# A selective-scan layer and a linear-attention layer: softplus chain and du moved three slots, diagonals of B through DRAM, one state's inflow on GpSimd

## Chip, cores and metric

The kernel runs on one core of one Trainium2 chip. The metric is the device time of one execution in microseconds (us). Below, PE is TensorE, DVE is VectorE, ACT is ScalarE, POOL is GpSimd and SP is SyncE, whose queue issues most DMAs.

## The reference

The input x is [2, 512, 64, 64] in float32, two images of 4096 tokens with 512 channels. Two layers follow each other; each takes the group norm of x, computes a layer of it and adds x again. The first is a Mamba layer with 1024 inner channels, 16 states and a rank of 32 for delta. Only its core matters here:

```python
x_dbl = xs @ x_proj_w.T                       # xs: [tokens, 1024], after conv and SiLU
dt, Bm, Cm = x_dbl[..., :32], x_dbl[..., 32:48], x_dbl[..., 48:]
delta = softplus(dt @ dt_proj_w.T + dt_proj_b)
A = -exp(A_log)                               # [1024, 16]
def step(h, inp):                             # over the 4096 tokens
    dA = exp(d_t[..., None] * A)
    dBu = (d_t * u_t)[..., None] * b_t[:, None, :]
    h = dA * h + dBu
    y = einsum('bdn,bn->bd', h, c_t)
y = (y + u * D_skip) * silu(z)
```

The second layer is a linear attention of 8 heads. The change does not touch it.

## The kernel before

**Chunks, tiles, slots.** The first layer goes over the tokens in 16 chunks of 512. A chunk is made of 8 tiles (j, 128 inner channels each), and a tile of 16 states (n). One state of one tile is a slot, so a chunk has 128 slots. The functions `scalar_chunk`, `vector_chunk`, `gpsimd_chunk`, `tensor_chunk` and `sync_chunk` write the queue of their engine slot by slot; the engines then run freely and meet at semaphores. Three things are laid over one another: the scan of chunk c, the front of chunk c+1 (norm, input projection, convolution, the projection to dt, B and C) and the output projection of chunk c-1. The tables of numbers at the head of the file (`OUT_MM`, `IN_MM`, `SP_LN`, `DU`, ...) say in which slot each piece stands. Chunks 1 to 14 run all three in a loop; chunk -1 is a front alone, chunk 0 has no output projection, chunk 15 has no front.

**A slot of the scan.** ACT makes the decay exp(delta * A) two slots ahead (L444). The inflow delta * u * B is made in one of two ways. For the ten states of `BY_TENSOR`, PE multiplies the transposed delta * u (`du_t`) with a diagonal matrix that holds the state's row of B (`b_diag`), four 128x128 matmuls into one of three PSUM banks, also two slots ahead (L742); a matmul of this type is two records in the profile, so a group is eight. For the six states of `BY_VECTOR`, DVE multiplies a copy of du with the broadcast row `b_rows` (L647), and then the decay goes to the PSUM bank. DVE scans (L659) into a ring of four buffers `hs`; POOL multiplies with `c_rows` into a ring of four buffers `hc` (L704); PE adds the sixteen products up by transposing matmuls three slots later (L846).

**The three banks.** `ring_bank(n)` deals the banks to the slots. Two other uses take a turn in the ring: the sum over the states of the tile before, transposed back (`Y_BACK`, L718), after slot `Y_AFTER`, and the transpose of du (`DU_TURN`, L725), after slot `DU_AFTER`. Behind such a turn the bank of a slot was free one scan later than else: `scans_before` gives 2 in place of 3, which for slot n means that its producer, two slots ahead, waits for the end of scan n-2 and not n-3. With `DU_AFTER` = 13 these are the slots 6, 7 (PE's groups) and 14, 15 (ACT's decays).

**The softplus chain.** During tile j the delta of tile j+1 is made: ACT Abs and Relu in slot 0, Exp in 1, two additions in 2 and 3 (`SP_ROUND`), POOL subtracts in 4 (`SP_REST`, L672), ACT takes Ln in 6 (`SP_LN`, L536, with a load of ACT's function table before it and another before the next decay), POOL adds in 8 (L676), subtracts in 9 (L681) and makes `du` in 10 (L690). PE transposes `du` in slot 12 (L725), ACT copies it to `du_t` in 13 (L540), and PE's groups for states 0 and 1 of tile j+1 stand in slots 14 and 15. `du_t` has two buffers.

**Rows and diagonals of B.** At slot 102 (`DBL`) ACT has B and C of the next chunk in `sq`. SP stores them to DRAM (L400) and loads them back, broadcast over the partitions, as `b_rows` (L408) and `c_rows` (L411), each row when its last user of the present chunk is done. For the diagonals PE transposes the rows (`B_TURN`, L751) and DVE multiplies an identity with them, one instruction a state, in the ten `BY_TENSOR` slots of tile 7 (L630).

Of the kernel before, what the change touches and what calls it, by code (L numbers as in the profile page):

```python
# [28 lines left out]
BY_TENSOR = (0, 1, 3, 4, 6, 7, 9, 10, 12, 13)  # L29
N_V, N_T = len(BY_VECTOR), len(BY_TENSOR)  # L30
# [3 lines left out]
Y_AFTER, DU_AFTER = 5, 13  # L34
# [94 lines left out]
def mamba_and_linear_attention(nc, x, ln_w, ln_b, in_proj, conv_w, conv_b, x_proj, dt_proj, dt_b, a_log, d_skip,  # L129
# [6 lines left out]
    bc_d = nc.dram_tensor("b_and_c_rows", [2 * STATE, T], FP32).ap()  # L136

    outer = ExitStack()
    with outer:
# [11 lines left out]
        with layer0:  # L151
# [1134 lines left out]
```

## Time and profile before

| | before |
|---|---|
| median of 3 runs | 5272.86 us (5270.67 to 5282.67) |
| the profiled execution | 5273.96 us, its span 5272.2 us |
| PE busy | 4649.4 us, 88% |
| DVE busy | 3947.5 us, 75% |
| POOL busy | 3635.1 us, 69% |
| ACT busy | 3497.5 us, 66% |
| first and last scan start | 186.0 us and 4479.9 us |

The sum of such shares hides the stages: up to 186 us stand the setup and the front of chunk 0, then 16 chunks of scan, and from about 4480 us the second layer. The start of a scan of state 0 marks a tile's beginning; the windows in the section of rows below are cut there.

### The profile page before, as it was taken

Reading aid. Unit: us, or ns where it says so; the run is one execution under the profiler, and the core shown is the slowest. Engines: PE = TensorE matmul, PEld = TensorE weight load, DVE = VectorE, ACT = ScalarE, POOL = GpSimd, SP = SyncE. Lnnn points to the kernel's source line nnn. Section 1 sums busy time; section 2 is a strip of 40 time slices with the busy share of each in tenths; the row PEclk is TensorE's granted clock in tenths of the full one; section 3 lists DMA queues with packets and bytes.
Section 4 is the critical chain, followed back from the end, with each engine's and each line's share of the span. In section 5 each row is a group of like instructions: output and inputs, shape, how many; then the busy total and the mean of one; then the engine's idle time right before and its main releaser. Section 6 shows DMA issues by size and latency. Waiting matters only on the chain. (4 is left out here: it accounts for less than half of the span.)

```text
span 5272.2 us, 90572 instructions
## 1 busy us (share of the span) xinstructions
PE 4649.4 (88%) x26392; PEld 3440.3 (65%) x26392; DVE 3947.5 (75%) x4317; ACT 3497.5 (66%) x6211; POOL 3635.1 (69%) x2906
## 2 busy tenths in 40 slices
PE   1798989898989898989898989999898988798998
PEld 0566666666666666666666666666666667586786
DVE  4788979898988888888888898989798988212212
ACT  1676767676767676777777777767676766463663
POOL 1477778777777777777777777777777789332432
PEclk8899999999999999999999999999999999999999
DMA  5102020201010201010101001010102010323313
GB/s 191 53 1 65 5 66 5 62 9 62 9 62 9 62 9 58 13 58 13 58 13 47 24 29 41 20 49 13 58 4 67 4 59 7 116 64 104 104 56 112
DMA packets 119824, 245.61 MB, mean 47 GB/s; under 512 B 10496, under 2 KB 11648, under 8 KB 117728
## 3 DMA queue, kind: packets, MB, share of 16 engines
q1 hardware_dynamic: 110816, 222.30, 12.9%
q10 hardware_dynamic: 8448, 16.78, 0.9%
q8 instruction: 237, 3.88, 0.3%
q14 instruction: 323, 2.65, 0.2%
HBM read 204.44 MB, written 34.60 MB: 45 GB/s over the span
## 5 line engine op out<-in xcount | busy, mean ns | idle before, releaser
L704 POOL TENSOR_TENSOR hc<-hs,c_rows 128x512 f32<-128x512 f32 x2048 | 2598.1, 1278 | 931.9 <-DVE hs L659 456.7
L659 DVE TENSOR_TENSOR_SCAN hs<-da,carry,bank 128x512 f32<-128x512 f32 x1280 | 1630.9, 1274 | 213.7 <-PE bank L742 110.4
L742 PE MATMUL bank<-b_diag,du_t 128*128 128x128 f32 x10240 | 1425.2, 284 | 282.3 <-ACT du_t L540 183.9
L742 PEld LDWEIGHTS bank<-b_diag,du_t 128*128 128x128 f32 x10240 | 1287.6, 197 | 347.4 <-issue 178.2
L846 PEld LDWEIGHTS bank<-identity,hc 128*128 128x128 f32 x8192 | 1016.9, 144 | 664.4 <-issue 558.3
L846 PE MATMUL bank<-identity,hc 128*128 128x128 f32 x8192 | 1251.3, 277 | 17.0 <-ACT sp_l L548 12.3
L444 ACT ACTIVATE da<-delta,neg_a 128x512 f32<-128x512 f32 x1280 | 906.1, 716 | 192.0 <-DVE hs L659 190.4
L659 DVE TENSOR_TENSOR_SCAN hs<-bank,carry,hs 128x512 f32<-128x512 f32 x768 | 962.3, 1266 | 0.5
L444 ACT ACTIVATE bank<-delta,neg_a 128x512 f32<-128x512 f32 x768 | 526.3, 685 | 555.0 <-DVE hs L659 443.0
L1017 POOL TENSOR_TENSOR xg_low<-xg,xg_high 128x512 fp32r<-128x512 f32 x192 | 248.5, 1295 | 473.3 <-ACT xg_high L1041 465.7
L647 DVE TENSOR_TENSOR hs<-bank,b_rows 128x512 f32<-128x512 f32 x768 | 518.3, 675 | 73.2 <-POOL hc L704 56.1
L832 PE MATMUL bank<-xs,w_out 128*128 (+1 forms) x1024 | 534.7, 626 | 29.9 <-issue 27.6
L782 PE MATMUL bank<-xn,w_in 128*128 (+1 forms) x1024 | 525.1, 599 | 23.5 <-DVE xs L594 12.4
L814 PE MATMUL bank<-xn,w_in 128*128 (+1 forms) x1024 | 524.9, 594 | 0.0
L424 ACT ACTIVATE carry<-hs,keep_now 128x2 f32<-128x2 f32 x1008 | 292.6, 290 | 241.5 <-DVE hs L659 238.7
L588 DVE SCALAR_TENSOR_TENSOR bank<-raw,w_conv,bank 128x512 f32<-128x512 f32 x384 | 289.6, 754 | 96.3 <-ACT bank L495 87.2
L832 PEld LDWEIGHTS bank<-xs,w_out 128*128 128x128 f32 x1024 | 188.4, 201 | 190.0 <-issue 184.6
L672 POOL TENSOR_TENSOR sp_w<-sp_w,sp_e 128x512 f32<-128x512 f32 x128 | 163.3, 1276 | 159.6 <-ACT sp_w L532 159.5
L814 PEld LDWEIGHTS bank<-xn,w_in 128*128 128x128 f32 x1024 | 174.6, 191 | 123.0 <-issue 122.4
L1041 ACT ACTIVATE xg<-xl,gn_bias,gn_scale 128x512 f32<-128x512 f32 x192 | 155.4, 809 | 137.5 <-DMA xl<-x 125.3
L1130 DVE COPY ek_t<-l_bank 128x512 f32<-128x512 f32 x64 | 44.3, 692 | 219.2 <-PE l_bank L1205 219.2
L609 DVE SCALAR_TENSOR_TENSOR xs<-xs,skip,bank 128x512 f32 (+1 forms) x128 | 94.5, 739 | 143.5 <-PE bank L718 143.5
(160 smaller groups left out, 5882.5 us busy)
## 6 DMA issues: line engine op xcount, KB each, us to landing
c_rows<-b_and_c_rows SPq DMA_DIRECT2D x256, 256.0 KB, 3.5
xl<-x SPq DMA_DIRECT2D x48, 1024.0 KB, 5.6
b_rows<-b_and_c_rows SPq DMA_DIRECT2D x96, 256.0 KB, 3.6
c_rows<-in_x SPq DMA_DIRECT2D x8, 2048.0 KB, 8.2
xn<-in_x ACTq DMA_DIRECT2D x16, 1024.0 KB, 7.4
xres<-in_x SPq DMA_DIRECT2D x64, 256.0 KB, 3.1
x<-xres SPq DMA_DIRECT2D x64, 256.0 KB, 2.0
out<-keys SPq DMA_DIRECT2D x16, 1024.0 KB, 5.0
```

What stands on the lines that cost most here:

```text
L424: act.activation(carry[:, col:col + 2], hs[:, col % H_RING:col % H_RING + 2, T - 1], ACT.Copy, scale=keep_now[:, 0:1]).then_inc(carried, 1)
L444: act.activation(x_ps[ring_bank(nn)][:, :] if nn in BY_VECTOR else da[:, nn % X_RING, :], delta[:, jn % 2, :], ACT.Exp, scale=neg_a[:, jn, ...
L588: dve.scalar_tensor_tensor(in_ps[t][:, :], raw[:, TAPS - 1 - s:TAPS - 1 - s + T], w, in_ps[t][:, :], ALU.mult, ALU.add).then_inc(conv_step, 1)
L647: dve.tensor_tensor(hs[:, nn % H_RING, :], du_ps[:, :], b_rows[:, v, :], ALU.mult).then_inc(dbu_ready, 1)
L659: dve.tensor_tensor_scan(hs[:, n % H_RING, :], decay, inflow, carry[:, STATE * j + n:STATE * j + n + 1], ALU.mult, ALU.add).then_inc(h_rea ...
L704: pool.tensor_tensor(hc[:, n % HC_RING, :], hs[:, n % H_RING, :], c_rows[:, n, :], ALU.mult).then_inc(hc_ready, 1)
L742: mm = pe.matmul(x_ps[ring_bank(nn)][:, q * P:(q + 1) * P], du_t[:, jn % 2, q * P:(q + 1) * P], b_diag[:, w, q, :], start=True, stop=True)
L782: mm = pe.matmul(in_ps[t][:, :], w_in[:, ct, t * P:(t + 1) * P], xn[:, f % 2, ct, :], start=ct == 0, stop=ct == CT - 1)
L814: mm = pe.matmul(pb[:, :], w_in[:, ct, lo:lo + P], xn[:, c % 2, ct, :], start=ct == 0, stop=ct == CT - 1)
L832: mm = pe.matmul(pout[:, :], w_out[:, k, ct * P:(ct + 1) * P], xs[:, o % 2, k, :], start=k == 0, stop=k == JT - 1)
L846: mm = pe.matmul(y_ps[:, q * P:(q + 1) * P], hc[:, ns % HC_RING, q * P:(q + 1) * P], identity[:, :], start=ns == 0 and q == 0, stop=ns == ...
L1017: pool.tensor_tensor(xg_parts[1][:, u, ct, :], xg[:, ct % 2, :], xg_parts[0][:, u, ct, :], ALU.subtract).then_inc(lowered, 1)
```

## The change

- `DU_AFTER` goes from 13 to 11. The chain moves: Exp of the softplus into slot 0, the additions into 1 and 2, POOL's subtraction into 3, Ln into 4, POOL's sum into 5, its second subtraction into 6, du into 8, PE's transpose of du into 10 and ACT's copy to `du_t` into 11. Ln now writes over `sp_e`, so it waits for POOL's subtraction, which reads `sp_e`; before it wrote `sp_l` and waited for the transpose of y. The SiLU gate of POOL goes from slot 7 to 9, the Tanh of z from 10 to 11. Slots 12 and 13 (PE's groups) now have the late bank, and 14 and 15 no longer.
- `du_t` has two buffers in both kernels; only the slot of the copy changes.
- The diagonals come by DMA. Setup zeroes `b_diag` on POOL and stores it as the blank of a DRAM tensor `b_diagonals`. Each chunk, SP writes the nine rows of B onto the diagonals in DRAM and loads the nine [128 x 512] blocks back. PE's turn (L751) and DVE's ten multiplications (L630) are gone.
- State 3 leaves `BY_TENSOR` for `BY_POOL`: POOL multiplies du with a broadcast row, two slots ahead, into the ring of `hs`, and the decay of state 3 goes to the bank.

```diff
 BY_VECTOR = (2, 5, 8, 11, 14, 15)
-BY_TENSOR = (0, 1, 3, 4, 6, 7, 9, 10, 12, 13)
+BY_TENSOR = (0, 1, 4, 6, 7, 9, 10, 12, 13)
+BY_POOL = (3,)
-Y_AFTER, DU_AFTER = 5, 13
+Y_AFTER, DU_AFTER = 5, 11
...
-    return 2 if Y_AFTER < n <= Y_AFTER + 2 or n > DU_AFTER else 3
+    return 2 if n - Y_AFTER in (1, 2) or n - DU_AFTER in (1, 2) else 3
...
-DT_MM, SP_ABS, SP_EXP, SP_ROUND, SP_LN, SP_REST, SP_SUM, SP_DELTA = 14, 0, 1, 3, 6, 4, 8, 9
-DU, DU_TURN, DU_T, DU_COPY = 10, DU_AFTER - 1, DU_AFTER, 15
-Z_MM, Z_TANH, Z_SILU = (2, 3, 6, 9), 10, 12
-Y_COPY, Y_BACK, Y_SKIP, Y_GATE = 3, Y_AFTER - 1, Y_AFTER + 1, 7
+DT_MM, SP_ABS, SP_EXP, SP_ROUND, SP_LN, SP_REST, SP_SUM, SP_DELTA = 14, 0, 0, 2, 4, 3, 5, 6
+DU, DU_TURN, DU_T, DU_COPY = 8, DU_AFTER - 1, DU_AFTER, 15
+Z_MM, Z_TANH, Z_SILU = (2, 3, 6, 9), 11, 12
+Y_COPY, Y_BACK, Y_SKIP, Y_GATE = 3, Y_AFTER - 1, Y_AFTER + 1, 9
...
+                    sp.wait_ge(diag_blank, 1)
+                    sp.dma_start(diag_d.rearrange("w q (p c) -> p (w q) c", p=P),
+                                 b_diag[:, :, :, :].rearrange("p w q c -> p (w q) c")).then_inc(diag_zeroed, 16)
...
                         sp.dma_start(bc_d, bc_rows).then_inc(bc_stored, 16)
+                        for w, n in enumerate(BY_TENSOR):
+                            wait(sp, diag_loaded[w], 16 * f)
+                            settle(sp, sp_fence)
+                            sp.dma_start(diag_d[w:w + 1, :, 0:P * P:P + 1],
+                                         bc_rows[n:n + 1, :].rearrange("a (q p) -> a q p", p=P),
+                                         allow_slow_non_contiguous=True).then_inc(diag_stored, 16)
                         sp.wait_ge(bc_stored, 16 * (f + 1))
                         settle(sp, sp_fence)
+                        sp.wait_ge(diag_stored, 16 * N_T * (f + 1))
...
+                            if n in BY_TENSOR:
+                                w = BY_TENSOR.index(n)
+                                wait(sp, dbu_mm, N_T * (JT * (c + 1) - 1) + w + 1)
+                                sp.dma_start(b_diag[:, w, :, :], diag_d[w].rearrange("q (p c) -> p q c", p=P)
+                                             ).then_inc(diag_loaded[w], 16)
...
                                 if n == SP_LN:
-                                    wait(act, y_back, tile)
-                                    act.activation(sp_l[:, :], sp_e[:, :], ACT.Ln, bias=one).then_inc(sp_ln, 1)
+                                    act.wait_ge(sp_rest, nt + 1)
+                                    act.activation(sp_e[:, :], sp_e[:, :], ACT.Ln, bias=one).then_inc(sp_ln, 1)
...
-                            if front and j == JT - 1 and n in BY_TENSOR:
-
-                                w = BY_TENSOR.index(n)
-                                dve.wait_ge(b_turned, f + 1)
-                                wait(dve, dbu_mm, N_T * (tile if scan else 0) + (w + 1 if scan else 0))
...
-                                dve.tensor_tensor(b_diag[:, w, :, :],
...
+                            if scan and n + 2 in BY_POOL:
+                                nn = n + 2
...
+                                pool.tensor_tensor(hs[:, nn % H_RING, :], du[:, :], b_rows[:, ROWS.index(nn), :],
+                                                   ALU.mult).then_inc(pool_dbu, 1)
```

PE's queue at the end of a tile of chunk 0, before. The groups of states 12 and 13 (`bank<-b_diag,du_t`) come first, then the transpose of du, a sum over the states (`bank<-identity,hc`), and the group of state 0 of the next tile:

```order
L742 MATMUL bank<-b_diag,du_t 128x128 x4
L846 MATMUL bank<-identity,hc 128x128 x4
L742 MATMUL bank<-b_diag,du_t 128x128 x4
L846 MATMUL bank<-identity,hc 128x128 x4
L725 MATMUL bank<-identity,du 128x128 x4
L846 MATMUL bank<-identity,hc 128x128 x8
L742 MATMUL bank<-b_diag,du_t 128x128 x4
L802 MATMUL bank<-dt_rows,w_dt 128x512
```

The same place of PE's queue in the changed kernel, where the groups are L775, the sums L870 and the transpose of du L760:

```order
L760 MATMUL bank<-identity,du 128x128 x4
L775 MATMUL bank<-b_diag,du_t 128x128 x4
L870 MATMUL bank<-identity,hc 128x128 x4
L775 MATMUL bank<-b_diag,du_t 128x128 x4
L870 MATMUL bank<-identity,hc 128x128 x12
L775 MATMUL bank<-b_diag,du_t 128x128 x4
L826 MATMUL bank<-dt_rows,w_dt 128x512
```

The transpose of du now stands ahead of the groups of states 12 and 13, and between them and the first group of the next tile stand three sums.

POOL's queue over one tile of chunk 0, before (`hc<-hs,c_rows` is the product of a slot, the others are the softplus chain, du and the gate `xs<-xs,zs`):

```order
L672 TENSOR_TENSOR sp_w<-sp_w,sp_e 128x512
L704 TENSOR_TENSOR hc<-hs,c_rows 128x512 x3
L697 TENSOR_TENSOR xs<-xs,zs 128x512
L704 TENSOR_TENSOR hc<-hs,c_rows 128x512
L676 TENSOR_TENSOR delta<-delta,sp_l 128x512
L704 TENSOR_TENSOR hc<-hs,c_rows 128x512
L681 TENSOR_TENSOR delta<-delta,sp_w 128x512
L704 TENSOR_TENSOR hc<-hs,c_rows 128x512
L690 TENSOR_TENSOR du<-delta,xs 128x512
L704 TENSOR_TENSOR hc<-hs,c_rows 128x512 x10
```

and in the changed kernel, where the products are L739:

```order
L732 TENSOR_TENSOR hs<-du,b_rows 128x512
L739 TENSOR_TENSOR hc<-hs,c_rows 128x512 x2
L698 TENSOR_TENSOR sp_w<-sp_w,sp_e 128x512
L739 TENSOR_TENSOR hc<-hs,c_rows 128x512 x2
L702 TENSOR_TENSOR delta<-delta,sp_e 128x512
L739 TENSOR_TENSOR hc<-hs,c_rows 128x512
L707 TENSOR_TENSOR delta<-delta,sp_w 128x512
L739 TENSOR_TENSOR hc<-hs,c_rows 128x512 x2
L717 TENSOR_TENSOR du<-delta,xs 128x512
L739 TENSOR_TENSOR hc<-hs,c_rows 128x512
L724 TENSOR_TENSOR xs<-xs,zs 128x512
L739 TENSOR_TENSOR hc<-hs,c_rows 128x512 x8
```

Six instructions stand among the products of slots 1 to 9 where five stood in slots 4 to 10; the new one is `hs<-du,b_rows`.

## Rows read from the trace of the kernel before

**Rows 1.** Windows, chunk 7's eight tiles: length, busy per engine, PEclk, DMA share, GB/s

```profile
2081.23:2119.76 38.53, 35.35 (x189) 24.86 (x190) 27.81 (x27) 23.45 (x41) 25.07 (x20) 0.91 0.24 75
2119.76:2157.47 37.71, 32.57 (x173) 22.26 (x172) 30.30 (x33) 27.20 (x45) 25.99 (x21) 0.95 0.05 15
2157.47:2190.49 33.02, 33.02 (x204) 24.61 (x203) 27.72 (x30) 24.86 (x47) 27.97 (x23) 1.00 0.02 9
2190.49:2221.86 31.37, 29.84 (x171) 20.95 (x170) 28.96 (x32) 21.52 (x40) 25.01 (x20) 1.00 0.03 10
2221.86:2254.81 32.95, 31.85 (x197) 23.60 (x196) 31.65 (x36) 26.21 (x51) 25.91 (x21) 1.00 0.00 1
2254.81:2290.05 35.24, 31.30 (x189) 22.57 (x187) 32.32 (x37) 28.08 (x55) 27.82 (x23) 1.00 0.00 1
2290.05:2321.09 31.04, 26.61 (x165) 20.39 (x164) 26.22 (x29) 21.84 (x40) 24.94 (x20) 0.95 0.01 3
2321.09:2352.92 31.83, 25.32 (x170) 20.87 (x170) 29.20 (x35) 19.70 (x34) 26.56 (x22) 0.94 0.54 160
```

**Rows 2.** Waits in chunks 1 to 14 (442.9:4254.0): us in total, times, longest

```profile
PE bank L742 <- ACT du_t L540: 152.8, 84, 3.1
...
DVE hs L659 <- PE bank L742: 99.9, 113, 4.4
...
PE bank L742 <- DVE hs L659: 80.4, 108, 1.8
```

**Rows 3.** Groups of instructions, whole span: busy us, mean ns, idle before

```profile
L742 PE MATMUL bank<-b_diag,du_t 128*128 128x128 f32 x10240 | 1425.2, 284 | 282.3 <-ACT du_t L540 183.9 <-DVE hs L659 95.6
...
L630 DVE TENSOR_TENSOR b_diag<-identity,bank 128x512 f32<-128x512 f32 x160 | 107.3, 675 | 17.8 <-PE bank L742 17.1 <-PE bank L751 0.7
```

**Rows 4.** Timeline, end of tile 6 of chunk 7: start, us, engine, line

```profile
2313.90 0.65 PE L725 MATMUL bank<-identity,du 128*128 128x128 f32 x4 [1.70 <-POOL du L690]
...
2317.68 0.58 ACT L540 ACTIVATE du_t<-bank 128x512 f32<-128x512 f32 x1
...
2318.38 2.07 PE L742 MATMUL bank<-b_diag,du_t 128*128 128x128 f32 x8 [2.66 <-ACT du_t L540]
```

**Rows 5.** Timeline, ACT in tile 4 of chunk 7

```profile
2236.17 1.28 ACT L536 ACT_TABLE_LOAD   x1
...
2239.50 0.72 ACT L444 ACTIVATE da<-delta,neg_a 128x512 f32<-128x512 f32 x1
```

**Rows 6.** Timeline, SP's queue from slot 102 of chunk 7

```profile
2303.22 0.33 SPq L400 DMA_DIRECT2D b_and_c_rows<-sq  x1
2324.51 2.33 SPq L411 DMA_DIRECT2D c_rows<-b_and_c_rows  x2
```

**Rows 7.** The page's DMA queues and issues: KB each, us to landing

```profile
q1 hardware_dynamic: 110816, 222.30, 12.9%
...
c_rows<-b_and_c_rows SPq DMA_DIRECT2D x256, 256.0 KB, 3.5
...
c_rows<-in_x SPq DMA_DIRECT2D x8, 2048.0 KB, 8.2
```

**Rows 8.** DMA issues of two small weights: KB each, us to landing

```profile
b_conv<-in_conv_b SPq DMA_DIRECT2D x1, 4.0 KB, 6.7
...
skip<-in_d_skip SPq DMA_DIRECT2D x1, 4.0 KB, 6.1
```

**Rows 9.** Timeline, SP's queue in the setup

```profile
10.49 0.43 SPq L231 DMA_DIRECT2D b_conv<-in_conv_b  x1
...
11.44 0.43 SPq L233 DMA_DIRECT2D skip<-in_d_skip  x1
```

**Rows 10.** Timeline, end of chunk -1

```profile
170.29 0.33 SPq L400 DMA_DIRECT2D b_and_c_rows<-sq  x1
...
172.00 0.80 SPq L411 DMA_DIRECT2D c_rows<-b_and_c_rows  x2
...
183.78 2.07 PE L742 MATMUL bank<-b_diag,du_t 128*128 128x128 f32 x8 [0.69 <-ACT du_t L540]
```

More of the change, by code:

```diff
@@ L42, in scans_before @@
 def scans_before(n):
-    return 2 if Y_AFTER < n <= Y_AFTER + 2 or n > DU_AFTER else 3
+    return 2 if n - Y_AFTER in (1, 2) or n - DU_AFTER in (1, 2) else 3
+assert Y_AFTER + 3 not in BY_TENSOR and DU_AFTER + 3 not in BY_TENSOR
 NORM, MEAN, CENTER = (3, 4, 6, 7), (6, 8, 11, 12), 15
@@ L172, in mamba_and_linear_attention @@
             c_rows = sb("c_rows", [P, STATE, T], layer0)
-            b_rows = sb("b_rows", [P, N_V, T], layer0)
+            b_rows = sb("b_rows", [P, len(ROWS), T], layer0)
             b_diag = sb("b_diag", [P, N_T, BLOCKS, P], layer0)
@@ L264, in _ @@
                                        channel_multiplier=-1).then_inc(consts, 1)
+                    pool.memset(b_diag[:, :, :, :], 0.0).then_inc(diag_blank, 1)
                     pool.wait_ge(w_in_loaded, 16)
@@ L329, in mamba_and_linear_attention @@
             c_loaded = [sem(f"c_loaded{n}") for n in range(STATE)]
-            b_loaded = [sem(f"b_loaded{v}") for v in range(N_V)]
+            b_loaded = [sem(f"b_loaded{v}") for v in range(len(ROWS))]
+            pool_dbu = sem("pool_dbu")
             dt_mm = sem("dt_mm")
@@ L343, in mamba_and_linear_attention @@
             du_turned, du_t_ready, du_copied = sem("du_turned"), sem("du_t_ready"), sem("du_copied")
-            b_turned, diag_ready = sem("b_turned"), sem("diag_ready")
+            diag_stored, diag_loaded = sem("diag_stored"), [sem(f"diag_loaded{w}") for w in range(N_T)]
             dbu_mm = sem("dbu_mm")
@@ L440, in scalar_chunk @@
                                     act.wait_ge(delta_ready, tile + 2)
-                                wait(act, h_ready, step + (3 - scans_before(nn) if nn in BY_VECTOR else 0) if scan else 0)
-                                if nn == Y_AFTER + 3 and nn in BY_VECTOR:
+                                wait(act, h_ready, step + (0 if nn in BY_TENSOR else 3 - scans_before(nn)) if scan else 0)
+                                if nn == Y_AFTER + 3 and nn not in BY_TENSOR:
                                     wait(act, y_skip, tile)
-                                act.activation(x_ps[ring_bank(nn)][:, :] if nn in BY_VECTOR else da[:, nn % X_RING, :],
+                                if nn == DU_AFTER + 3 and nn not in BY_TENSOR:
+                                    wait(act, du_t_ready, tile + 2 if (front if j == 7 else scan) else 0)
+                                act.activation(da[:, nn % X_RING, :] if nn in BY_TENSOR else x_ps[ring_bank(nn)][:, :],
                                                delta[:, jn % 2, :], ACT.Exp,
@@ L506, in scalar_chunk @@
                                 wait(act, dt_mm, JT * f)
+                                wait(act, diag_stored, 16 * N_T * f)
                                 wait(act, bc_stored, 16 * f)
@@ L516, in scalar_chunk @@
                                     wait(act, delta_ready, nt)
+                                    wait(act, sp_sum, nt)
                                     act.activation(sp_e[:, :], pb[:, :], ACT.Abs,
@@ L546, in scalar_chunk @@
                                 act.wait_ge(n_summed, STATE * tile)
-                                act.wait_ge(sp_sum, tile)
+                                wait(act, y_back, tile - 1)
                                 act.activation(sp_l[:, :], y_ps[:, :], ACT.Copy).then_inc(y_copied, 1)
@@ L652, in vector_chunk @@
                                     dve.wait_ge(dbu_ready, N_V * tile + BY_VECTOR.index(n) + 1)
+                                    decay, inflow = x_ps[ring_bank(n)][:, :], hs[:, n % H_RING, :]
+                                elif n in BY_POOL:
+                                    dve.wait_ge(pool_dbu, N_P * tile + BY_POOL.index(n) + 1)
                                     decay, inflow = x_ps[ring_bank(n)][:, :], hs[:, n % H_RING, :]
@@ L688, in gpsimd_chunk @@
                                 wait(pool, du_copied, nt)
+                                wait(pool, pool_dbu, N_P * nt)
                                 settle(pool, pool_fence)
@@ L736, in tensor_chunk @@
                                 if jn == 0:
-                                    pe.wait_ge(diag_ready, N_T * cn + w + 1)
+                                    pe.wait_ge(diag_loaded[w], 16 * (cn + 1))
                                 wait(pe, h_ready, step + 3 - scans_before(nn) if scan else 0)
-                                if nn == Y_AFTER + 3:
-                                    wait(pe, y_skip, tile)
                                 for q in range(BLOCKS):
@@ L744, in tensor_chunk @@
                                 mm.then_inc(dbu_mm, 1)
-                            if front and slot == B_TURN:
-                                pe.wait_ge(dt_split, f + 1)
-                                pe.wait_ge(xs_ready, JT * (f + 1))
-                                settle(pe, pe_fence)
-                                for q in range(BLOCKS):
-                                    mm = pe.transpose(pa[:, q * 2 * STATE:(q + 1) * 2 * STATE],
-                                                      bc_rows[:, q * P:(q + 1) * P],
-                                                      identity[3 * RANK:, 3 * RANK:])
-                                mm.then_inc(b_turned, 1)
                             if front and slot in MEAN:
```

33 lines of the change are left out of this document (21 added, 12 removed).

## The prediction

> **What bounds the kernel now.** I first cut one middle chunk into its eight tiles, since the page's shares average stages with different limits. In [rows 1] each row is a tile of 31 to 38.5 us; the eight sum to 271.7 us, and 14 chunks of the loop are like this one. Read the engine that comes nearest to the tile's length. In tiles 0 to 2 it is PE (35.35 of 38.53, 32.57 of 37.71, 33.02 of 33.02). In tiles 3 to 5 PE and DVE stand side by side (29.84 and 28.96 of 31.37, 31.85 and 31.65 of 32.95, 31.30 and 32.32 of 35.24). In tiles 6 and 7 nothing is full: PE has 26.61 and 25.32, POOL 24.94 and 26.56, of 31.04 and 31.83; there the in-order queues wait for each other. Over the chunk PE has 245.85 us, DVE 234.18, POOL 209.27.
>
> Then the waits of chunks 1 to 14 [rows 2]. PE's largest is for ACT's copy `du_t`, 152.8 us in 84 waits, 10.9 us a chunk. PE's groups wait 80.4 us for scans, 5.7 us a chunk; these are the groups whose bank comes free late. DVE waits 99.9 us for groups, 7.1 us a chunk. [rows 4] show the first kind: PE idles 1.70 us until POOL's du is there, transposes it at 2313.90, ACT copies at 2317.68, and the group of state 0 starts at 2318.38 after 2.66 us of idle PE. The copy stands one slot ahead of its first user, which is too near.
>
> **The change part by part.**
>
> *du three slots forward.* Between copy and first group now stand three slots, each about 2.1 us (271.7 / 128). The longest such wait was 3.1 us [rows 2], so nearly all of the 10.9 us a chunk of PE's idle time goes. It is worth its full amount only where PE sets the end.
>
> *One group of ten fewer.* A group has 1425.2 / 1280 = 1.11 us of PE [rows 3]; one less in each tile is 8.9 us a chunk. B's turn on PE, a half group's length, goes too.
>
> *No diagonals on DVE.* 10 x 0.675 = 6.75 us less in tile 7 [rows 3].
>
> *One product more on POOL.* POOL's instructions take 25.07 / 20 = 1.25 us [rows 1], so 1.25 us a tile, 10 us a chunk. POOL then has 219 of some 260 us. Six additions now stand in slots 1 to 9: 15 instructions, 18.8 us, in nine slots of 2.0 us, so POOL just keeps pace there, and the ring of four `hs` buffers lets it lag by two or three slots before DVE waits.
>
> *The late bank moves to slots 12 and 13.* PE must now wait for the end of scan 10 and of scan 11 before two groups that had one scan more. Behind them in PE's queue stand the sums of `hc`, for which POOL waits through its ring, and matmuls of the projections. The trace has the same construction at slots 6 and 7, and it costs PE at most 5.7 us a chunk. Bounds: nothing, where PE is late anyway (tiles 0 to 2), and another 5.7 us of PE with DVE's 7.1 us behind it. I take a third of the former, 2 us.
>
> *Ln waits for POOL's subtraction.* ACT's queue holds Ln, then the decays of states 7 and 8 and the carries; DVE waits for the decays. From the table load before Ln to the end of the next decay it is 2236.17 to 2240.22, 4.0 us [rows 5], in either kernel. ACT runs two slots ahead, 4.2 us. So a wait of up to about 1 us is free, since ACT is at most 80% busy [rows 1]; I take 0 and keep 1.2 us a tile as a bound (below).
>
> *Diagonals through DRAM, each chunk.* After the store of the rows at 2303.22 the first load goes out at 2324.51 only, since it waits for its last user [rows 6]; the first group that needs the new diagonals starts about 2.7 us ahead of the next chunk's first scan (2321.09 - 2318.38, rows 1 and 4), at 2352.9 - 2.7 = 2350.2. Of these 47 us a load takes 3.5 us [rows 7] and a store's landing 1.7 us (170.29 to 172.00, [rows 10]), which leaves 42 us for nine stores of 512 single elements. b_conv landed at 10.49 + 6.7 = 17.19 and skip at 11.44 + 6.1 = 17.54 [rows 8, 9]: two transfers of 128 short rows in 0.35 us, with 16 engines 8 packets per 0.175 us, 22 ns each. If a 4-byte packet takes that, the 4608 packets take 6.3 us on 16 engines or 25 us on four (the outer length of the pattern, so the least to expect); hidden either way. Behind the stores SP's queue holds the loads of `b_rows` and `c_rows`, for which DVE and POOL wait in the next chunk. The loads grow from 22 to 32 a chunk, two in a slot of 2.1 us, each issued in less than 0.5 us; each lands some 15 slots before its use.
>
> *The same at chunk -1.* Here nothing hides it. The store goes out at 170.29, the first group starts at 183.78 [rows 10]. Nine more issues of 0.47 us ((11.44 - 10.49) / 2, [rows 9]), landing 1.7 and a load 3.5 give 179.7: no loss. With 25 us of packets: 200.5, a loss of 17. I take 8.
>
> *Setup.* 2.36 MB of zeros go ahead of the eight loads of x, which move 2.1 MB in 8.2 us [rows 7]: 9 us, and DVE's statistics wait for these loads.
>
> A rule of the Trainium skill speaks against the diagonals. *DMA: Bandwidth & Descriptors*, "Why a DMA increments its semaphore by 16 and not by 1", says that a DMA runs on the largest number of engines up to 16 that divides the slowest dimension, and its "Rules for kernel authors" that a strided last dimension becomes one descriptor per element. The stores have the shape 4x128x1, so by this they would run on four engines with 128 packets each, which is the 25 us case and not the 6.3 us case; the sum holds by both.
>
> **The sum.** For each tile: the fullest engine after the change, plus what of today's idle time stays when the wait for `du_t` is gone.
>
> - Tile 0: PE 34.2 + 2.5 = 36.7 (now 38.5). Tile 1: 31.5 + 4.5 = 36.0 (37.7). Tile 2: 31.9 + 0.5 = 32.4 (33.0).
> - Tile 3: DVE 29.0 + 1.0 = 30.0 (31.4). Tile 4: 31.65 + 0.9 = 32.6 (32.95). Tile 5: 32.3 + 1.4 = 33.7 (35.2).
> - Tile 6: POOL or DVE 26.2 + 2.9 = 29.1 (31.0). Tile 7: POOL 27.8 + 1.4 = 29.2 (31.8).
>
> Together 259.7, which is 12 us less a chunk; the 2 us of the new late banks are in the idle parts that I left. The ceiling is PE's own saving, 10.9 + 8.9 = 19.8 us. Fifteen chunks (-1's front excepted, and 0 taken like the others): -180. The last chunk has no front and PE is light, so there POOL's 1.25 us a tile shows: up to +10, I take +5. Setup +9, first diagonals +8. Sum: -158. The profiled execution took 5273.96 us, 1.1 above the median of the runs; from the median 5272.9 it gives 5115.
>
> **The rivals.**
>
> *Waits take the gain's place (faster, but by little).* The late banks cost their upper bound, 5.7 us of PE or 7.1 us of DVE a chunk, so 5 to 6 of 12 us remain: 5273 - 15 x 5.5 + 22 = 5212. For it: tiles 6 and 7, where PE is ahead and so would hit these waits. Against: in tiles 0 to 5 PE is late, not early.
>
> *More than PE's saving (lower still).* Moving `du_t` also ends waits that DVE and POOL have behind PE; 20 us a chunk and more: below 4990.
>
> *The change moves waits around and nothing else.* 5262 to 5283. Against it: 8.9 us of work leave the fullest engine.
>
> *The stores are late (slower).* If a 4-byte store takes as long as the average packet of the queue, 0.129 x 16 x 5272.2 / 110816 = 98 ns [rows 7], and only four engines work, nine stores take 1152 x 98 ns = 113 us, 71 us more than there is room for. All engines then stop at the head of each chunk: 5115 + 15 x 71 = 6180. On 16 engines the same packets take 28 us and are hidden. It decides from (42 + 12) / 1152 = 47 ns a packet on four engines; short rows took 22 ns, though they were reads and not stores.
>
> *POOL or Ln sets the pace (slower).* If POOL lags by more than its slack in slots 1 to 9, Ln comes late, and decay 7 with it. This costs a tile what it is late; it cancels the gain from 158 / 128 = 1.2 us a tile on, and at 1.5 us gives 5115 + 192 = 5307. Against: POOL idles 62 of 271.7 us now.
>
> **How the numbers follow.** A difference under 0.2% can't be told from none here. The forecast (7 to 20 us a chunk, 5000 to 5200) has 0.66; waits in the gain's place 0.12 (5200 to 5262); more than PE's saving 0.04; no change 0.05; late stores 0.08; POOL or Ln 0.05. Faster is 0.66 + 0.12 + 0.04 = 0.82, same 0.05, slower 0.13. The range 4990 to 5270 leaves out the fastest case, both slow ones and some of no change, 0.2 in all.
>
> **What would show it.** Right: PE's wait for `du_t` nearly gone, groups 1152 in place of 1280, a chunk of 258 to 262 us, tile 7 shortened most, SP's first loads still waiting for their users and not for the stores. Wrong: PE or ACT waiting for a load of `b_diag` at the head of chunks, new waits of PE's groups for scans well over 11 us a chunk, a decay late behind Ln, or DVE waiting for POOL's `hs`.

## The result and the profile after

| | before | after |
|---|---|---|
| median | 5273.56 us (5270.67 to 5282.67, 4 runs) | 5233.87 us (5230.1 to 5240.14, 4 runs) |
| span of the profiled execution | 5272.2 us | 5231.1 us |
| first scan starts | 186.0 us | 203.8 us |
| chunks 1 to 14, mean | 272.4 us | 268.6 us |
| chunk 0 / chunk 15 | 257.0 / 224.6 us | 253.2 / 217.1 us |
| last scan's end to the end | 791.1 us | 796.5 us |

The changed kernel is faster, by 0.8%; the ratio is 0.992 (0.9908 to 0.9932). One run of e10, below, took 5389.1 us in a slower state of the chip and is left out of its figures. The prediction had 5115 and a gain of 158 us; the gain is 40 us. By stages, from the spans: +17.8 us at the start, -3.8 in chunk 0, 14 x -3.8 = -53 in the loop, -7.5 in chunk 15, +5.4 behind the scans, together -41.

The windows of chunk 7's tiles in the changed kernel (columns as in [rows 1]; length, then busy of PE, PEld, DVE, ACT, POOL):

```profile
2073.24:2111.57 38.33, 34.47 (x184) 23.53 (x185) 28.12 (x28) 23.59 (x41) 26.29 (x21) 0.96 0.26 89
2111.57:2148.28 36.71, 30.57 (x166) 21.53 (x165) 30.41 (x33) 28.32 (x47) 27.26 (x22) 0.95 0.04 15
2148.28:2179.39 31.11, 31.11 (x190) 22.94 (x189) 27.76 (x31) 24.09 (x46) 28.53 (x24) 1.00 0.03 10
2179.39:2212.11 32.72, 31.03 (x179) 21.85 (x178) 28.85 (x32) 22.13 (x42) 26.92 (x23) 1.00 0.03 9
2212.11:2244.73 32.62, 30.36 (x178) 21.38 (x178) 31.66 (x37) 25.57 (x49) 26.88 (x22) 1.00 0.01 2
2244.73:2279.68 34.95, 30.98 (x182) 21.91 (x180) 32.40 (x37) 27.75 (x56) 28.96 (x24) 1.00 0.00 0
2279.68:2307.02 27.34, 25.15 (x162) 19.01 (x161) 25.51 (x27) 20.50 (x37) 25.74 (x21) 1.00 0.06 5
2307.02:2338.91 31.89, 23.67 (x159) 19.21 (x156) 24.19 (x25) 20.56 (x37) 28.69 (x24) 0.94 0.71 207
```

Tiles 2 and 6 fell as forecast or by more (33.0 to 31.1 us, 31.0 to 27.3). Tiles 0, 1, 4 and 5 hardly moved, tile 3 became longer (31.4 to 32.7), tile 7 stayed (31.8 to 31.9) although DVE has 5 us less to do in it. In this chunk PE's busy time fell in every tile but 3. One profiled chunk varies against the mean: over chunks 1 to 14 the eight tiles take 39.2, 38.8, 31.3, 32.7, 32.6, 35.0, 27.4 and 31.8 us, and before 37.9, 38.0, 33.0, 31.4, 32.9, 35.2, 31.8 and 32.1.

Tile 1 has the same instructions in every chunk and does not take the same time. Its windows in chunks 12 and 13 of the changed kernel, and one group of PE in each:

```profile
3454.07:3495.16 41.09, 34.35 (x163) 23.36 (x162) 30.49 (x32) 29.98 (x50) 27.15 (x22) 0.83 0.04 13
3726.34:3763.05 36.71, 29.23 (x165) 20.35 (x164) 30.40 (x32) 28.32 (x47) 27.29 (x22) 1.00 0.04 15
```

```profile
3486.13 2.08 PE L775 MATMUL bank<-b_diag,du_t 128*128 128x128 f32 x8 [2.48 <-DVE hs L685]
...
3756.71 1.16 PE L775 MATMUL bank<-b_diag,du_t 128*128 128x128 f32 x8 [3.22 <-DVE hs L685]
```

DVE's work is the same in both. What differs is TensorE's granted clock, 0.83 and 1.00 in the mean: in chunk 12 it was at the lower of its two levels (1.2 GHz, not 2.4) for part of the tile, and PE was busy 5 us longer. Over the 14 chunks the tile takes 36.7 us where the clock is 0.95 or more (5 chunks), 37.8 to 39.4 us at 0.91 and 0.87 (4 chunks), and 40.8 to 41.1 us at 0.83 (5 chunks). In the kernel before it takes 37.7 us at 0.95 or more (10 chunks) and 38.7 to 39.0 at 0.91 (4 chunks), and the clock is never lower. So at a high clock the tile did fall, by 1.0 us; the lower clock puts 2.1 us on it in the mean, where it was 0.3. Tile 0's clock fell too, from 0.96 to 0.92 in the mean. Tiles 2 to 6 of the changed kernel are at 1.00 throughout.

The waits of chunks 1 to 14 of the changed kernel, to be read beside [rows 2]:

```profile
PE bank L775 <- DVE hs L685: 278.0, 224, 3.2
...
DVE zs L636 <- ACT zs L585: 119.2, 84, 2.3
...
DVE hs L670 <- ACT carry L453: 79.9, 79, 2.3
...
DVE hs L685 <- issue: 61.1, 13, 5.3
DVE hs L685 <- PE bank L775: 54.9, 77, 2.6
```

PE's 152.8 us for `du_t` are gone. In their place PE's groups wait 278.0 us for scans, 19.9 us a chunk where it was 5.7. DVE has three waits that it hardly had: for ACT's Tanh of z (8.5 us a chunk), for the carry of states 4 and 5 before its product for state 8 (5.3 of 5.7 us a chunk), and one of 4.7 us on average that no semaphore explains, 13 times, once for each turn of the loop.

The end of chunk -1, a timeline of SP and the engines (start, us, engine, line):

```profile
173.84 0.33 SPq L411 DMA_DIRECT2D b_and_c_rows<-sq  x1
...
174.28 17.58 SPq L417 DMA_DIRECT2D b_diagonals<-sq  x9
...
198.71 0.39 SPq L437 DMA_DIRECT2D b_diag<-b_diagonals  x1
...
201.62 2.05 PE L775 MATMUL bank<-b_diag,du_t 128*128 128x128 f32 x8 [15.80 <-DMA b_diag<-b_diagonals]
```

The first load goes out 24.9 us after the first store, and PE's first group waits for the landing until 201.62, where it stood at 183.78 before [rows 10]. The windows of these stores, of those in chunk 7 and of the loads at its end (the last three columns are PEclk, DMA share and GB/s), and the page's queue and issues:

```profile
175.00:197.00 22.00, 1.19 (x5) 0.71 (x4) 0.00 (x0) 9.75 (x14) 5.05 (x4) 0.57 0.24 49
2296.00:2312.00 16.00, 12.16 (x88) 9.78 (x87) 15.41 (x16) 11.46 (x23) 15.84 (x13) 1.00 0.11 2
2315.00:2339.00 24.00, 17.52 (x119) 14.62 (x117) 16.29 (x18) 12.60 (x22) 20.71 (x17) 0.92 0.91 277
```

```profile
q1 hardware_dynamic: 268080, 266.91, 16.2%
...
c_rows<-b_and_c_rows SPq DMA_DIRECT2D x256, 256.0 KB, 7.3
...
b_diag<-b_diagonals SPq DMA_DIRECT2D x144, 256.0 KB, 7.2
```

The Trainium skill's rule on the number of engines (*DMA: Bandwidth & Descriptors*, "Why a DMA increments its semaphore by 16 and not by 1") would put these stores on four engines. No run here shows it: the share is a mean over 16 engines; it is 0.24 where other transfers run beside the stores (49 GB/s) and 0.11 in chunk 7, where hardly anything else does (2 GB/s). At the end of a chunk the loads keep them busy to 0.91, and a row of B or C lands in 7.3 us, not 3.5 [rows 7].

### The profile page after: what moved, and what is told of

Same layout as the page of the kernel before. It is cut to its first block and busy times, and to the rows that moved or that the text cites. A ratio compares the mean times of both kernels' runs of the same rounds, so it can differ in the third digit from the quotient of the medians.

```text
span 5231.1 us, 88902 instructions
## 1 busy us (share of the span) xinstructions
PE 4528.0 (87%) x25304; PEld 3301.3 (63%) x25304; DVE 3861.5 (74%) x4157; ACT 3494.4 (67%) x6211; POOL 3782.1 (72%) x3035
## 5 line engine op out<-in xcount | busy, mean ns | idle before, releaser
L739 POOL TENSOR_TENSOR hc<-hs,c_rows 128x512 f32<-128x512 f32 x2048 | 2589.6, 1279 | 707.2 <-DVE hs L685 473.5
L775 PE MATMUL bank<-b_diag,du_t 128*128 128x128 f32 x9216 | 1285.2, 284 | 349.0 <-DVE hs L685 325.1
L685 DVE TENSOR_TENSOR_SCAN hs<-da,carry,bank 128x512 f32<-128x512 f32 x1152 | 1465.7, 1272 | 159.9 <-PE bank L775 85.8
L870 PEld LDWEIGHTS bank<-identity,hc 128*128 128x128 f32 x8192 | 1008.3, 143 | 707.3 <-issue 580.6
L775 PEld LDWEIGHTS bank<-b_diag,du_t 128*128 128x128 f32 x9216 | 1147.7, 196 | 430.5 <-DVE hs L685 391.4
L870 PE MATMUL bank<-identity,hc 128*128 128x128 f32 x8192 | 1232.8, 277 | 50.8 <-ACT sp_l L581 33.9
L685 DVE TENSOR_TENSOR_SCAN hs<-bank,carry,hs 128x512 f32<-128x512 f32 x896 | 1118.7, 1266 | 18.6 <-ACT bank L475 12.2
L475 ACT ACTIVATE da<-delta,neg_a 128x512 f32<-128x512 f32 x1152 | 822.7, 714 | 298.4 <-DVE hs L685 296.9
L475 ACT ACTIVATE bank<-delta,neg_a 128x512 f32<-128x512 f32 x896 | 612.2, 683 | 207.1 <-DVE hs L685 205.1
```

The costliest lines, as they stand in the source:

```text
L475: act.activation(da[:, nn % X_RING, :] if nn in BY_TENSOR else x_ps[ring_bank(nn)][:, :], delta[:, jn % 2, :], ACT.Exp, scale=neg_a[:, jn, ...
L685: dve.tensor_tensor_scan(hs[:, n % H_RING, :], decay, inflow, carry[:, STATE * j + n:STATE * j + n + 1], ALU.mult, ALU.add).then_inc(h_rea ...
L739: pool.tensor_tensor(hc[:, n % HC_RING, :], hs[:, n % H_RING, :], c_rows[:, n, :], ALU.mult).then_inc(hc_ready, 1)
L775: mm = pe.matmul(x_ps[ring_bank(nn)][:, q * P:(q + 1) * P], du_t[:, jn % 2, q * P:(q + 1) * P], b_diag[:, w, q, :], start=True, stop=True)
L870: mm = pe.matmul(y_ps[:, q * P:(q + 1) * P], hc[:, ns % HC_RING, q * P:(q + 1) * P], identity[:, :], start=ns == 0 and q == 0, stop=ns == ...
```

## The experiments

Each kernel was timed beside the kernel before on the same chip, so ratios are compared; the changed kernel's is 0.992. A us value is a median. Two accounts stand against each other: that the fuller use of DVE now limits the tiles, so that a wait taken away comes back as another, and that single new waits and transfers, each at its own place, ate the gain. The letters of the theories are those of the expectations. A third account, that TensorE's clock took part of the gain, was not among them; what the traces say of it stands with e9 and e13.

**e1: the SiLU of z one slot later.**

```diff
-Z_MM, Z_TANH, Z_SILU = (2, 3, 6, 9), 11, 12
+Z_MM, Z_TANH, Z_SILU = (2, 3, 6, 9), 11, 13
```

> The changed kernel with the SiLU of z on VectorE one slot later (13 in place of 12), so that two slots and not one lie behind ScalarE's Tanh. Theory P (placement): VectorE's wait for the Tanh, 8.5 us a chunk in the changed kernel, goes, and half or more of it shows: 5150 to 5190 us. Theory V (VectorE and its other partners set the pace, PE's saving has nowhere to go): the wait moves to another partner, 5225 to 5240 us. Theory M (memory traffic at the chunk's head took the gain): no change from 5234 us, and the head of each chunk stays as it is.

5220.1 us, ratio 0.990 (0.9879 to 0.9921). The wait for the Tanh is gone, and DVE's waits of e1 in chunks 1 to 14 show where it went:

```profile
DVE hs L685 <- PE bank L775: 100.1, 143, 2.6
...
DVE xres L652 <- PE bank L856: 49.6, 28, 2.9
...
DVE hs L670 <- POOL hc L739: 32.4, 44, 1.1
```

DVE's wait for PE's groups grew from 54.9 to 100.1 us, and new ones for PE's output projection and POOL's products came up. Its idle time fell from 38.0 to 37.3 us a chunk only. Theory V has it right, with a small gain on top: 14 us by the medians and 11 by the ratios, whose intervals overlap. Tiles 3 and 5 are 0.7 and 0.9 us shorter, tiles 0 and 1 are 0.4 us longer each.

**e2 and e3: the diagonals by DMA alone, and everything but them.** e2 is the kernel before with the hunks of the diff on `diag_d`; e3 is the changed kernel without them:

```diff
-                            sp.dma_start(diag_d[w:w + 1, :, 0:P * P:P + 1],
...
-                                sp.dma_start(b_diag[:, w, :, :], diag_d[w].rearrange("q (p c) -> p q c", p=P)
...
+                                dve.tensor_tensor(b_diag[:, w, :, :],
```

> The kernel before with the diagonals of B laid by DMA (ten of them, no VectorE product and no turn on PE) and nothing else changed. Theory M: the first scan starts 18 to 20 us later and each chunk's head is 2 to 5 us longer, against at most 6.7 us of VectorE saved in tile 7, so the part alone is no gain: 5270 to 5310 us. Theory P or V: the traffic is harmless, tile 7 falls by 2 to 6 us, 5200 to 5250 us.

> The changed kernel with the diagonals made as before, by a turn on PE and nine products on VectorE in tile 7. Theory M: the first scan starts near 186 us, the pause at the chunk's head falls from 4.4 to about 1.8 us and xn lands in 7.4 us again; that gives 17.8 + 15 x 3 to 5 us back and costs 6.1 us of VectorE in tile 7 in part, so 5170 to 5220 us. Theory P or V: the products cost 3 to 6 us a chunk and only the start is won, 5250 to 5290 us.

e2: 5288.5 us, ratio 1.0025 (1.0015 to 1.0035), slower than the kernel before. e3: 5216.6 us, ratio 0.9887 (0.9868 to 0.9906), faster than the changed kernel. So the diagonals by DMA cost 13 to 17 us either way: the start comes 16 to 19 us late (203.8 against 187.4 us in e3), and what DVE saves in tile 7 does not arrive. In chunks 1 to 14 e3 and the changed kernel are even, 268.5 and 268.6 us. DVE's waits of e3, chunks 1 to 14:

```profile
DVE zs L614 <- ACT zs L563: 111.1, 84, 2.3
...
DVE hs L674 <- issue: 5.3, 4, 1.4
```

The pause at the loop's turn has shrunk, with nine products more on DVE. This row has only what is put down to no semaphore. DVE's whole idle time before the first scan after a turn, in the mean of the 13 turns, is 2.4 us before, 4.7 in the changed kernel and 1.3 in e3.

**e11: the stores kept, the loads left out.**

```diff
-                                sp.dma_start(b_diag[:, w, :, :], diag_d[w].rearrange("q (p c) -> p q c", p=P)
-                                             ).then_inc(diag_loaded[w], 16)
+                                sp.sem_inc(diag_loaded[w], 16)
```

> The changed kernel with the loads of the diagonals left out and their stores kept; TensorE multiplies with the zeros of the setup, so the inflow of nine states is zero. Theory M (the loads crowd the chunk's head): the pause at the loop's end falls from 4.4 us to 2 or less, the row loads land in 3.5 us and not 7.2, and about 3 us a chunk, 40 to 50 us, come back; the first scan still starts 14 to 18 us late. If the element-wise stores are what crowds: pause and landings stay.

5186.6 us, ratio 0.9836 (0.9817 to 0.9855), some 45 us below the changed kernel. Its windows of tile 7 of chunk 7 and of tile 0 before it:

```profile
2283.18:2313.00 29.82, 23.54 (x159) 19.09 (x157) 24.17 (x26) 20.56 (x37) 28.68 (x24) 0.94 0.62 177
2047.48:2084.50 37.02, 35.46 (x184) 24.05 (x185) 28.02 (x28) 23.55 (x41) 26.28 (x21) 0.91 0.24 80
```

Tile 7 takes 29.8 us (31.9) and tile 0 37.0 (38.3), the other six are the same to 0.5 us in the mean over the chunks. The DMA share in tile 7 is 0.62, not 0.71. Rows land in 4.9 us (7.3), DVE's pause falls to 21.9 us in all, or from 4.7 to 3.0 us a turn with all that ends it. The loads' crowding is worth 3.0 us a chunk (268.6 against 265.6), and it sits in the tiles on both sides of the turn: tile 7 is 1.6 us shorter in the mean, tile 0 2.0. Part of tile 0's may be the clock, which is 0.95 there and not 0.92. The element stores, which stay, leave the first scan late (199.9 us).

**e4: Ln back in slot 6.**

```diff
-DT_MM, SP_ABS, SP_EXP, SP_ROUND, SP_LN, SP_REST, SP_SUM, SP_DELTA = 14, 0, 0, 2, 4, 3, 5, 6
+DT_MM, SP_ABS, SP_EXP, SP_ROUND, SP_LN, SP_REST, SP_SUM, SP_DELTA = 14, 0, 0, 2, 6, 3, 7, 7
```

> The changed kernel with Ln in slot 6 again and both of GpSimd's delta instructions in slot 7; du stays in slot 8. Theory P: VectorE's wait for the carry of states 4 and 5, which stands behind Ln and its two table loads in ScalarE's queue, 5.3 us a chunk, goes: 5160 to 5210 us, unless du comes late now (PE would then wait for du). Theory V: 5225 to 5245 us. Theory M: no change.

5280.5 us, ratio 1.0011 (1.0001 to 1.002): the whole gain is gone. The waits of e4:

```profile
PE bank L760 <- POOL du L717: 61.3, 42, 2.3
...
DVE hs L670 <- ACT carry L453: 3.9, 9, 1.0
```

The wait for the carry before the product fell from 79.9 to 3.9 us as expected, but PE now waits 61.3 us (18.2) for du and the chunk is 2.6 us longer. The place of Ln trades one wait for a worse one.

**e5 and e6: the schedule alone, and state 3 on POOL alone.** e5 has ten states on PE and diagonals by DVE under the new tables; e6 has the old tables, and `BY_POOL = (3,)`. Ln writes over its own input in both.

> The kernel before with the schedule of the changed one alone (DU_AFTER 11, the chain forward, Ln over its own input); ten states on TensorE, diagonals by VectorE. If the schedule brought the gain: 5210 to 5235 us. If it only moves waits (theory V): 5255 to 5280 us. TensorE should show its wait for the du^T copy gone and new waits for scans in its place.

> The kernel before with state 3's inflow on GpSimd alone, the schedule as before except that Ln writes over its own input and so waits for GpSimd's subtraction. If TensorE set the pace (the prediction's step), its 8.9 us a chunk show by half or more: 5170 to 5210 us. If VectorE and the fixed chains do (theory V): 5240 to 5270 us, and TensorE idles more.

e5: 5221.9 us, ratio 0.9895 (0.9879 to 0.9912). Alone it gives at least as much as all three parts together; the intervals (up to 0.9912, and from 0.9908) just touch. Its waits:

```profile
PE bank L752 <- DVE hs L671: 295.2, 280, 3.2
...
DVE zs L614 <- ACT zs L563: 110.6, 84, 2.3
```

e6: 5251.2 us, ratio 0.9944 (0.9928 to 0.9961), 29 us of the 142 us that PE is spared in 16 chunks. Its waits:

```profile
PE bank L763 <- ACT du_t L550: 164.4, 89, 3.1
...
PE bank L763 <- DVE hs L673: 122.1, 140, 1.8
...
DVE hs L673 <- PE bank L763: 60.7, 80, 2.8
```

PE waits more for scans (122.1 us, was 80.4) and for `du_t` (164.4, was 152.8), DVE less for groups (60.7, was 99.9): the freed time of PE became idle time. In chunk 15, where POOL is the fullest engine, e6 is 7.3 us longer (231.9 against 224.6).

**e8, e9, e10 and e14: the same probes on both kernels.** The PE probe leaves out three of the four matmuls of state 4's group. I had put that at 8 x 0.83 = 6.7 us of PE a chunk; the busy time of the groups fell by 84.0 us in all (e8) and 89.5 us (e9), which is 5.3 and 5.6 us a chunk, 0.7 a tile. The DVE probe makes the product of state 15 on a quarter of the columns. It then takes 0.27 us and not 0.68, which is 3.3 us of DVE a chunk, 0.4 a tile.

```diff
-                                for q in range(BLOCKS):
+                                for q in range(1 if nn == 4 else BLOCKS):
...
-                                dve.tensor_tensor(hs[:, nn % H_RING, :], du_ps[:, :], b_rows[:, v, :],
+                                cols = slice(0, P if nn == 15 else T)
+                                dve.tensor_tensor(hs[:, nn % H_RING, cols], du_ps[:, cols], b_rows[:, v, cols],
```

> The kernel before with three of the four matmuls of state 4's group left out (so that three quarters of this state's inflow is wrong), which takes 0.83 us a tile or 6.7 us a chunk from TensorE and adds nothing anywhere. If TensorE is the bound in tiles 0 to 5, as the prediction has it: 15 x 4 to 6.7 us less, 5175 to 5215 us. Theory V: under 25 us less, above 5250 us.

> The changed kernel with three of the four matmuls of state 4's group left out (three quarters of this state's inflow is wrong): 6.7 us of TensorE a chunk less. On the kernel before the same edit gave 50 us. If TensorE is no longer what most tiles wait for (theory V): 0 to 25 us below the changed kernel's 5234. If it still is: another 45 us or more.

> The changed kernel with VectorE's inflow product of state 15 on 128 of its 512 columns (three quarters of this state's inflow is stale): about 0.4 to 0.5 us of VectorE a tile, 3.5 us a chunk. If VectorE sets the pace (theory V): 30 to 55 us below 5234. If TensorE does: under 15 us.

> The kernel before with VectorE's inflow product of state 15 on 128 of its 512 columns (three quarters of this state's inflow is stale): 3.5 us of VectorE a chunk less. Taking 6.7 us of TensorE a chunk from the same kernel gave 50 us, 0.47 us for each. If both engines already set the pace together there (theory V): 15 to 30 us less. If TensorE did alone, as the prediction has it for tiles 0 to 2 and 5: under 12 us.

| work taken in 16 chunks | from the kernel before | from the changed kernel |
|---|---|---|
| PE, 84 and 90 us | 5229.9 us, 0.9906 (0.989 to 0.9923): about 50 us | 5222.4 us, 0.9902 (0.9884 to 0.9919): about 10 us |
| DVE, 52 us | 5270.5 us, 0.9987 (0.9975 to 0.9999): about 7 us | 5206.6 us, 0.9866 (0.9844 to 0.9889): about 28 us |

A microsecond of PE was worth 0.6 us before and 0.1 after; one of DVE 0.1 before and 0.5 after. e9's interval overlaps that of the changed kernel (0.9908 to 0.9932), so PE's 0.1 may be nothing.

These are sums over unlike tiles. The mean length of each tile over chunks 1 to 14, probe less kernel, from one profiled execution each:

| tile | 0 | 1 | 2 | 3 | 4 | 5 | 6 | 7 |
|---|---|---|---|---|---|---|---|---|
| PE probe, before (e8) | -0.4 | -0.7 | -0.7 | -0.7 | 0.0 | 0.0 | -0.6 | 0.0 |
| PE probe, changed (e9) | -0.4 | +1.2 | -0.6 | -0.7 | 0.0 | +0.1 | -0.1 | 0.0 |
| DVE probe, before (e14) | 0.0 | -0.3 | 0.0 | -0.2 | -0.4 | 0.0 | +0.1 | +0.1 |
| DVE probe, changed (e10) | +0.9 | -0.7 | 0.0 | -0.4 | -0.4 | -0.1 | -0.4 | -0.2 |

Before, PE set tiles 1, 2, 3 and 6, and tile 0 in part. In the changed kernel it still sets tiles 2 and 3. In tile 6 DVE has taken its place. In tile 1 sparing PE is worth nothing at a high clock (36.6 us at 0.95 in e9, 36.7 in the changed kernel), but e9's clock is lower there: 0.83 in eight chunks in place of five, 0.86 and not 0.90 in the mean. So the tile is 1.2 us longer with less to do, and without it a microsecond of PE would be worth 0.3. Whether PE's clock fell because PE had less work, or by the chance of one execution, is not shown. My expectation for e14 under theory V was wrong, since DVE set only tile 4 for certain before; with the change it gained tiles 3 (beside PE) and 6.

**e7 and e12: the parts that won, together.** e7 is e3 with the SiLU in slot 13, e12 is e5 with it.

> The changed kernel with both single edits that won: diagonals by VectorE, and the SiLU of z one slot later. If the two gains (17 and 14 us) add up: 5200 to 5206 us. If the second again only moves its wait: 5212 to 5220 us.

> The new schedule with the SiLU of z in slot 13, ten states on TensorE and diagonals by VectorE, so no DMA diagonals and nothing more on GpSimd. If state 3 on GpSimd is worth its place once the schedule is there: 10 us or more above the kernel that has all three (5203). If it is not: equal or lower, 5195 to 5210.

e7: 5203.5 us, ratio 0.986 (0.9841 to 0.9878). e12: 5201.6 us, ratio 0.9869 (0.9852 to 0.9885). The two gains of e7 add up; state 3 on POOL is worth nothing once the schedule is new.

**e13: the solid block of DVE in tile 1 split.**

```diff
-RSTD, NEWTON, SCALE, AFFINE = 24, 26, 27, 28
+RSTD, NEWTON, SCALE, AFFINE = 24, 26, 29, 30
```

> The new schedule alone with the SiLU in slot 13, and in tile 1 the norm's scaling (2.3 us of VectorE) moved two slots behind the four Newton steps (2.8 us). If VectorE's solid block there is what keeps tile 1 near 38 us while every engine has idle time: 1 to 3 us a chunk, 15 to 45 us below the kernel without the move (5202). If the sum of work or the waits elsewhere set tile 1: no change within 10 us.

5185.7 us, ratio 0.9829 (0.9812 to 0.9846), the fastest of the kernels that leave no work out. Tile 1 in e12, of chunk 7 and of chunk 11, then of chunk 7 in e13:

```profile
2084.43:2122.35 37.92, 31.87 (x171) 22.51 (x170) 30.48 (x32) 29.41 (x50) 25.91 (x21) 0.91 0.05 15
3157.35:3194.04 36.69, 31.66 (x173) 22.38 (x172) 30.40 (x32) 28.19 (x47) 26.08 (x21) 0.95 0.04 15
```

```profile
2078.43:2115.16 36.73, 31.85 (x183) 22.32 (x182) 30.41 (x33) 26.89 (x45) 26.12 (x21) 1.00 0.05 16
```

In chunk 7 the tile is 1.2 us shorter with the same DVE time (30.48 and 30.41 us), and the granted clock of TensorE in it is 1.00 in place of 0.91. The other chunks tell more. e12 has the solid block in every chunk, and in three of them the tile takes 36.7 us, as in e13; in the other eleven it takes 37.8 to 39.3. e13 has 36.7 to 37.0 in all fourteen. The mean clock of the tile is 0.91 in e12 and 0.96 in e13. So the block alone does not make the tile longer; with it the clock is lower in most chunks and the tile then takes longer. At a clock of 0.91 e13 still takes only 36.9 to 37.0 us, so where the low stretch falls matters as well. Why the clock falls in one chunk and not in the next, with the same instructions, is open.

## Why the prediction was right or wrong

**Right: the wait for `du_t`.** It went from 10.9 us a chunk to nothing, as computed, and tile 6, which had 2.6 us of it, fell by 4.5 us (forecast 1.9). But nearly all of it had stood in tiles 3 to 7. Tiles 0 to 2 had 0.5 us of it together, and the sum took 0.7 and 0.6 us of idle time off tiles 0 and 1.

**Right: the stores of the diagonals in the loop.** The timeline of SP at slot 102 of chunk 7 in the changed kernel:

```profile
2293.61 0.34 SPq L411 DMA_DIRECT2D b_and_c_rows<-sq  x1
2294.15 17.58 SPq L417 DMA_DIRECT2D b_diagonals<-sq  x9
2315.15 0.41 SPq L437 DMA_DIRECT2D b_diag<-b_diagonals  x1
```

From the first store to the first load it is 21.5 us, inside the 42 us that were worked out; 25 us was the estimate from the 22 ns rows. The rival of late stores did not happen in the loop. One sign of being right did not come: the first loads do wait for the stores, in all 16 chunks (us in total, times, longest):

```profile
SPq L374 <- DMA b_diagonals<-sq: 53.7, 16, 6.7
```

**Wrong in size: the first diagonals.** I took 8 us, half way between 0 and 17. The store goes out 3.6 us later than before (173.84, setup's share, which I had at 9) and the first scan 17.8 us later, so the diagonals cost 14.2. The upper bound was nearly right and should have been the term. The two errors cancel, 17 us forecast and 17.8 measured, and that is luck. So is the last chunk, below, which hides 12.5 us of what the loop lost.

**The step that failed: "the fullest engine after the change, plus what of today's idle time stays".** This sum gave 259.7 us a chunk, and the chunks take 268.6. Measured less forecast, tile by tile, it is +2.5, +2.8, -1.1, +2.7, 0.0, +1.3, -1.7 and +2.6 us. That is 14 x 9 = 125 us too little gain in the loop. The amount of work taken off PE was right; the two terms beside it were not.

*The idle time that stays.* Tiles 0 and 1 of chunk 7 had 3.2 and 5.1 us of PE idle time, and I carried these over a little reduced, 2.5 and 4.5; they rose to 3.9 and 6.1 (38.33 - 34.47, 36.71 - 30.57). Idle time is not a quantity that lasts. PE's waits for scans rose by 14 us a chunk, which is more than the 10.9 us of the removed wait. And the sum had no term for the clock. At a high clock tile 1 takes 36.7 us, near the 36.0 forecast; the lower clock puts 2.1 us on it, three quarters of what was missed there. Tile 0's clock fell as well; its loss is shared with the loads, below, and not told apart.

*Which engine is the fullest.* For tile 3 I took DVE (29.0 + 1.0 us), and PE is busy 31.0 of 32.7 us there; e9 shows that it still sets this tile. Tiles 2 and 3 together became 0.4 us shorter; the forecast had 2.0.

Of the 9 us a chunk, 3.0 come back when the loads are left out (e11), 2.1 are tile 1's clock, and 0.8 come back in e1. The rest is spread over the waits and not told apart.

The rival "waits take the gain's place" (5212) named the late banks. Of PE's 278 us of waits for scans, states 12 and 13, which have the late bank now, take 88 (36 before), and states 0 and 4 take 73 and 82. So its mechanism was a part of it, and its time near.

**Not foreseen: the loads at the chunk's head.** I checked that each load is issued long before its use, and took the traffic for harmless. The trace of the changed kernel shows the engines stop together when the loop turns (start, us, engine; the idle time before is in brackets):

```profile
2338.91 1.28 DVE L685 TENSOR_TENSOR_SCAN hs<-da,carry,bank 128x512 f32<-128x512 f32 x1 [4.49 <-issue]
...
2341.04 3.78 PE L856 MATMUL bank<-xs,w_out 128*128 x4 [4.73 <-issue]
...
2341.22 1.27 POOL L739 TENSOR_TENSOR hc<-hs,c_rows 128x512 f32<-128x512 f32 x1 [5.05 <-issue]
```

No semaphore ends these 4 to 5 us. At a turn DVE idles 4.7 us in the mean, 3.0 without the loads (e11), 1.3 without the diagonals by DMA (e3), but also 2.4 in the kernel before, whose DMA engines are no busier than e3's at this place (a share of 0.59 in the last 28 us of a chunk in both). So the loads lengthen the pause, and something in the new order shortens it; what it is made of is open. With the crowding of tile 7 and tile 0 it costs 3.0 us a chunk, 42 us in the loop, and eats what DVE saved in tile 7: -2.6 forecast there, -0.3 measured.

**Not foreseen: two distances of one slot.** I looked at the chain from ACT to POOL to PE, but not at what stands one slot apart after the move: the Tanh in 11 before the SiLU in 12, and the carry in 6 behind Ln in 4 before DVE's product in 7. They cost DVE 14 us of waiting a chunk; taking the first away gave 11 to 14 us in the whole run (e1), since another wait follows at once.

**The last chunk.** I put +5 us there for POOL and it took -7.5: the new schedule shortens it by 6.5 (218.1 us in e5), and POOL's product, +7.3 under the old tables (e6), costs nothing under the new ones (218.3 in e3).

**Still open.** The stretch behind the last scan is 5 to 7 us longer in the changed kernel and in e1, e3, e4, e6, e7, e10 and e11, 3 us in e2, and not (1.3 us or less) in e5, e8, e9, e12, e13 and e14. It has the same instructions everywhere. e9 differs from the changed kernel by three matmuls in a group of the first layer only, so neither POOL nor the diagonals explain it.

## What to carry to other kernels

When the profile shows two engines near the length of a stage, work taken from the fuller one is worth its price only until the other takes over; a probe that takes a little work from each engine, on a kernel whose output is of no interest, prices this in two runs. Read its answer stage by stage, since one stage can cancel the others. Look at the granted clock of a stretch, and at the same stretch in several turns of the loop, before you carry its idle time over: in tile 1 TensorE idled more after the change and its clock was lower too. Read the new order for distances of one slot, and not only for the chain that was moved. A transfer that is issued early enough for its own user still costs what it does to the other transfers, here at a loop's turn in a tile where 0.54 of the DMA engines' time was already in use [rows 1].

## What the hardware showed that was not expected

Writing 4608 elements of 4 bytes to DRAM from rows of one partition took 21.5 us in the loop and 24.9 us at the end of chunk -1, counted to the first load behind them: 4.7 and 5.4 ns an element in all. The estimate from the short rows, 22 ns an element on each of four engines, was 25 us. The DMA share was 0.11 while they ran in the loop.

The same 256 KB landed in 7.3 us where the DMA share was 0.91 and in 3.5 us before, with 32 loads of 256 KB (8.4 MB) in place of 22 (5.8 MB) per chunk.

The same tile with the same instructions took from 36.7 to 41.1 us in one execution, in step with TensorE's granted clock from 1.00 to 0.83. A group of PE took 1.16 us at the upper level and 2.08 at the lower.
